# Two-layer transformer on one core: first-layer attention right behind the q/k projection, its output projection at the end of the same slot

## What is computed

```python
xn = layernorm(x)                                  # 8 x 256 x 256
x  = x + attn0(xn) + ffn0(xn)
xn = layernorm(x)
x  = x + attn1(xn) + ffn1(xn)

attn0: 16 heads of 128, biases on q, k, v, causal mask, softmax, output projection 2048 -> 256
ffn0:  float8 operands, gelu(gate) * linear, 1024 hidden
attn1: 16 heads of 16, no mask, output projection 256 -> 256
ffn1:  Walsh-Hadamard transform, up and gate projections, silu(gate) * up,
       transform, down projection (1024 hidden)
```

## Time and profile before

| | |
|---|---|
| runs (3) | 956.63, 958.75, 959.01 us; median 958.75 |
| profiled execution | 958.63 us, its span 956.8 us |
| first block | to about 144 us of the span |
| slots 3 to 127 | from 158.9 to about 852 us |
| mean granted TensorE clock | 0.937 |

### The profile page before, as it was taken

One profiled execution on the slowest core, in us unless ns is written; L12 is line 12 of the kernel. 1 busy time (PEld: TensorE's weight loads), 2 busy tenths in 40 slices (PEclk: granted clock), 3 DMA queues, 4 the chain that ended last, 5 costly groups with the idle time before them and its releaser, 6 DMA issues.

```text
span 956.8 us, 21194 instructions
## 1 busy us (share of the span) xinstructions
PE 830.6 (87%) x7120; PEld 609.9 (64%) x7120; DVE 742.3 (78%) x2028; ACT 689.1 (72%) x1973; POOL 471.4 (49%) x734
## 2 busy tenths in 40 slices
PE   3555538999899999999999999999999999996763
PEld 1123225687677777777777777777777777764541
DVE  6988855766768788887878787878787878875684
ACT  2654625656669778887888888788778878884673
POOL 1443332412326565665666555656565656566452
PEclk9675778999999999999999999999999999998896
DMA  9543412212243456554564555455556554544454
GB/s 331 196 148 110 133 52 82 52 34 43 48 103 75 90 93 140 102 83 108 123 105 78 115 116 111 77 124 102 107 80 143 89 101 89 123 98 93 114 107 102
DMA packets 283179, 100.97 MB, mean 106 GB/s; under 512 B 241344, under 2 KB 281024, under 8 KB 281920
## 3 DMA queue, kind: packets, MB, share of 16 engines
q1 hardware_dynamic: 280368, 97.27, 45.9%
q10 hardware_dynamic: 2704, 2.36, 0.7%
HBM read 30.38 MB, written 10.49 MB: 43 GB/s over the span
## 4 chain that ended last, share of the span: by engine, by line
PE 68%; DVE 9%; ACT 3%; issue 2%; DMA 1%; POOL 1%; SPq 0%; POOLq 0%; DVEq 0%; ACTq 0%
PE ps L666 42%; PE ps L716 9%; PE ps L816 4%; PE ps L799 4%; PE ps L692 3%; DVE arena L660 2%; PE ps L825 2%; PE ps L801 2%; PE ps L729 2%; DVE arena L999 1%; ACT arena L655 1%; DMA arena<-arena 1%; ACT arena L875 1%; DVE arena L659 1%; DVE nb L1006 1%
## 5 line engine op out<-in xcount | busy, mean ns | idle before, releaser
L660 DVE SCALAR_TENSOR_TENSOR arena<-ps,bqk,arena 128x256 bf16<-128x256 f32 x416 | 187.4, 479 | 63.3 <-ACT arena L655 61.8
L666 PE MATMUL ps<-arena,wqkv 128*128 128x256 bf16 x1728 | 215.2, 275 | 6.5 <-PEq L210 6.5
L655 ACT ACTIVATE arena<-ps,bqk 128x256 bf16<-128x256 f32 x416 | 177.9, 466 | 30.0 <-PE ps L666 20.8
L666 PEld LDWEIGHTS ps<-arena,wqkv 128*128 128x128 bf16 x1728 | 161.7, 98 | 48.1 <-issue 28.3
L1174 POOL TENSOR_SCALAR arena<-arena,rc 128x128 f32<-128x128 f32 (+1 forms) x256 | 106.3, 428 | 174.4 <-DVE rc L1022 174.4
L875 ACT ACTIVATE arena<-arena,nb 128x128 f32<-128x128 f32 (+1 forms) x256 | 114.3, 447 | 90.0 <-DVE nb L999 89.4
L1165 POOL TENSOR_TENSOR arena<-arena 128x512 bf16<-128x512 f32 x107 | 124.8, 1167 | 69.8 <-ACT arena L654 69.8
L1181 POOL TENSOR_SCALAR arena<-arena,rc 128x256 f32<-128x256 f32 x256 | 120.1, 483 | 75.7 <-DVE rc L1026 75.7
L654 ACT ACTIVATE arena<-arena 128x384 bf16<-128x384 f32 (+1 forms) x256 | 136.6, 572 | 18.7 <-POOL arena L1181 9.8
L875 ACT ACTIVATE arena<-ps,nb 128x256 f32<-128x256 f32 x256 | 118.6, 473 | 13.3 <-DVE nb L1006 10.8
L716 PE MATMUL ps<-wo,arena 128*128 128x256 bf16 x768 | 105.6, 274 | 10.5 <-DVE arena L660 9.8
(11 more groups left out here) (98 smaller groups left out, 1286.4 us busy)
## 6 DMA issues: line engine op xcount, KB each, us to landing
arena<-scratch_qk SPq DMA_DIRECT2D x96, 64.0 KB, 2.2
arena<-arena SPq DMA_TRANSPOSE x256, 2.7
scratch_qk<-arena SPq DMA_DIRECT2D x32, 128.0 KB, 1.9
arena<-in_x SPq DMA_DIRECT2D x4, 512.0 KB, 8.6
arena<-in_w_gating SPq DMA_DIRECT2D x2, 1024.0 KB, 6.7
arena<-in_w_q SPq DMA_DIRECT2D x2, 1024.0 KB, 8.6
scratch_xT<-arena ACTq DMA_DIRECT2D x8, 256.0 KB, 6.4
arena<-in_w_k SPq DMA_DIRECT2D x2, 1024.0 KB, 6.4
```

The costliest lines, as they stand in the source:

```text
L655: return nc.scalar.activation(out, in_, ACT.Identity, bias=bias)
L660: return nc.vector.scalar_tensor_tensor(out=out, in0=in_, scalar=bias, in1=hi, op0=ALU.add, op1=ALU.subtract)
L666: last = nc.tensor.matmul(out, lhsT, rhs, start=(n == 0), stop=(n == len(steps) - 1))
```

## The change

TensorE's loop calls attend0 directly behind the q/k projection, and project_out0 at the end of the slot, and now for the head of the same slot (`s - 3`, where it was `s - 4`). The evictions in between, o0_high and o0_low, go from the head of the slot on ScalarE and VectorE to a place behind the eviction of q and k. x1_sum, which needs the last output projection of a sequence, goes to the head of VectorE's slot. up_gate waits for x1T_lo itself, which the wait in project_out0 had implied.

```diff
@@ up_gate
                 upto(pe, v0_lo, min(s // 2 + 1, NG0 // 2))
+                pe.wait_ge(x1T_lo, b + 1)
@@ pe_program
                 if s < NG0:
                     proj_qk0(s)
-                if 0 <= s - 4 < NG0:
-                    project_out0(s - 4)
+                if 0 <= s - 3 < NG0:
+                    attend0(s - 3)
...
-                if 0 <= s - 3 < NG0:
-                    attend0(s - 3)
                 for n in quads_in[s]:
                     attend1(n)
                 for n in downs_in[s]:
                     down(n)
+                if 0 <= s - 3 < NG0:
+                    project_out0(s - 3)
@@ act_program
-                if 0 <= s - 4 < NG0:
-                    o0_high(s - 4)
...
                 if s < NG0:
                     qk0_high(s)
+                if 0 <= s - 3 < NG0:
+                    o0_high(s - 3)
@@ dve_program
-                if 0 <= s - 4 < NG0:
-                    o0_low(s - 4)
+                for b in x1_in[s]:
+                    x1_sum(b)
...
                 if s < NG0:
                     qk0_low(s)
+                if 0 <= s - 3 < NG0:
+                    o0_low(s - 3)
                 for n in heads_in[s]:
                     rec_1(n)
-                for b in x1_in[s]:
-                    x1_sum(b)
```

## The result

The changed kernel takes **1008.32 us**, the median of three runs (1008.04 to 1009.23), where the kernel before takes 958.75 (956.63 to 959.01). The ratio is 1.053, 95% interval 1.051 to 1.055: slower by about 50 us. The profiled execution spans 1006.5 us, against 956.8.

The account below looks back on a forecast made before the run. TensorE, its matmuls following without a hole from slot 28, was taken to bound the kernel. Terms 19.7 + 4.4 + 0.5 + 2.6 + 22.2 - 2.5 = 46.9, plus 3 for the clock, on 958.6 gave 1009 us; range 980 to 1031.

Parts of the forecast that it names:

- Q: Moment a slot's q/k projection has been issued; output projection cannot start before Q + 2.45 with layer-1 heads, Q + 2.64 without.
- The fold slots: Slots 3, 5, 7 and 8 to 15, with fold matmuls behind the output projection's wait: 6.83 us each.
- slots 3 to 15: Early slots where the output projection waits for evicted heads: 88.0 us instead of 68.3, +19.7.
- rival 1: Waits stay in early slots and are absorbed later, as weight loads leave TensorE room: 984 us, 13%.
- Slots 23 to 27: up_gate and layer-1 projection pieces fill 23, 24, 27; 25 and 26 wait: +0.5 us, bounds -1 and +3.
- Rounds: Slots 32 to 127, six rounds of 16: 3.7 us a round, +22.2 in all.
- Places 12, 14 and 15: Slots of a round: 12 and 15 wait 0.64 us each; in 14 ScalarE has o1_high first, 0.7.
- 0.3 goes with the removed waits at a slot's head: In each round, a gain of 0.3 us from waits removed at the slot's head.
- Place 10: Slot 10 of a round: attend0 waits 1.0 us for its transfer, swallowing the wait for o0_low.
- Tail: Slot 128's 1.95 us wait and half clock go, x1_sum no longer behind a reciprocal: -2.5 us (0 to -5).
- The clock: Two falls of TensorE's clock, 1.5 us each, between none and ten: +3 us.
- rival 2: Clock falls at each of ten long waits: 1021 us, or 1030 if TensorE stays at 1.2 GHz through some folds; 13%.

Follow-up runs that it names:

- The experiment with the fold ahead: Changed kernel with plain instead of transposing probability transfers and the up/down projections' fold before the output projection on TensorE: 983.6 us, 1.027 of the kernel before.
- The experiment with the early attention alone: Changed kernel with plain transfers, output projection back one slot later behind the q/k projection, x1_sum back behind rec_1: 963.7 us, 1.006 of the kernel before.
- The control: Kernel before, with each transposing transfer of the probabilities replaced by two plain ones of the same bytes: 956.2 us, 0.998 of the kernel before.

## Why the prediction was right

Forecast 1009 us, measured 1008.3, and the direction, the mechanism and the place of the loss are those of the prediction. That the total agrees within 1 us is partly luck: the clock cost 3.2 us more than forecast, and the rounds lost 3.5 us less.

- **The wait.** The output projection at Q + 2.64 without heads and Q + 2.45 with them: measured Q + 2.63 and Q + 2.40. The fold slots: 6.83 predicted, 6.85 measured; a slot of 28 to 31 was to take 4.69 + 0.64 = 5.33 and takes 5.30. The total of slots 3 to 15 without clock falls was to be 88.0 and is 88.2; slots 16 to 22 without theirs take 37.21 - 1.42 = 35.8, with 35.9 forecast. The experiment with the fold ahead shows that these waits are the cause: with a cover of 1.74 us, 18.1 us of them vanish. The issue intervals of the earlier trace rows decide, and the waits were not caught up in the rounds: the prediction's rival 1, which drew its room from the 3.89 us of weight loads, would have given 984. The rule of the Trainium skill on which it leaned ("Perfetto Trace Analysis", Identifying the Most-Contended Engine) is not borne out here as far as weight loads go: their busy time stood at 83% of the slot where TensorE had no room at all. That section of the Trainium skill names the share of the peak matmul rate beside weight-load time; the prediction read only the second, and no run here tests the first.
- **Slots 23 to 27**: +1.1 where +0.5 stood, inside its bounds. Slots 23 and 24 gained 0.39 and 0.61 us, 25 and 26 lost 0.63 and 0.31, as sketched. But slot 27, which was to be filled past the wait, lost 1.15 us: attention waits 1.21 us for its transfer there, a wait that the prediction had in the rounds only.
- **Rounds**: 3.1 us each instead of 3.7. Places 12, 14 and 15 came out as sized (0.62, 0.78, 0.60 against 0.64, 0.7, 0.64), and so did 11 (0.27 against 0.3), 3 (0.40 against 0.5), and 2, 6 and 9 together (0.34 against 0.2 for 2, 9 and 13). What failed is the last term, "0.3 goes with the removed waits at a slot's head": it was worth 0.55 in place 0 and 0.34 in place 4. Both could have been read in the kernel before. From slot 32 to 127 the matmuls of its output projection wait five times, always in place 0, and the lengths (0.53, 0.88, 0.54, 0.53, 0.53) are what the change won there (0.57, 0.92, 0.57, 0.57, 0.58). In place 4 of all six rounds its weight loads wait 0.34 us for o0_low. Place 10 came out at 0.99 against 1.0, in part by luck: five rounds lost 0.77 to 0.98 us, one 1.77, and in two of the six the wait was for o0_low and not for the transfer. The first wait in place 0, and the first in place 4:

```profile
398.97 0.83 PE L716 MATMUL ps<-wo,arena 128*128 128x256 bf16 x6 [0.53 <-DVE arena L660]
...
330.88 0.55 PEld L716 LDWEIGHTS ps<-wo,arena 128*128 128x128 bf16 x6 [0.34 <-DVE arena L660]
```

- **The second cause in the rounds.** The prediction put the waits for the transfer beside those for the eviction. The experiment with the early attention alone bears it out: such waits stay when the output projection's wait is gone. In the changed kernel they are 4.8 us in all between 340 and 905 us, about a quarter of the 18.7 us that the rounds lost.
- **Tail**: -1.3 instead of -2.5. The wait of 1.95 us at slot 128 and its clock fall were both to go. Neither did: in the changed kernel the output projection of that slot waits 1.40 us, and a fall of the clock follows. The control has the wait without a fall, so the fall was not a fixed part of that place. The tails of the five traces lie between 100.0 and 103.8 us, so a difference of 1.3 says little.

```profile
907.88 0.83 PE L716 MATMUL ps<-wo,arena 128*128 128x256 bf16 x6 [1.40 <-DVE arena L660]
...
910.00:913.00 3.00, 3.00 (x18) 2.10 (x16) 0.87 (x3) 1.48 (x6) 1.61 (x3) 0.55 0.90 230
```

- **The clock**: four falls of 1.06 to 2.03 us, 6.2 us in all, where two of 1.5 stood. The number of falls was the wrong step. The prediction's rival 2 (a fall at each of the ten long waits) did not come true either: in the timeline nine waits of the output projection between 170 and 290 us last 1.8 us or more, and four of them are followed by a fall. The prediction's "read strictly, every one of the ten would fall" took more from the Trainium skill than is there: its "TensorE: Matmul & The Clock Gate", Part 1, puts a condition on the idle time and does not say that every wait brings a fall.
- **"DVE arena L660" before L716** was to be some 75 us or more in over 100 places, and is 117.2 in 142. The bound held, but it was loose: the view counts weight loads and matmuls, each with its own wait.
- **Before slot 3** the changed kernel is 1.4 us ahead, of which nothing was forecast. The new order starts only there. The five traces, whose kernels have the same programs up to that point, reach slot 3 between 157.51 and 158.94 us, so 1.4 us is the scatter of that stretch and no effect of the change.

## What to carry to other kernels

A step that is moved nearer to what it waits for costs its whole latency less what stands between; find the moment at which its input can be there (here the q/k eviction's start plus two of its operations plus 0.54 us) and subtract, slot kind by slot kind, since the slots with a cover cost nothing. If such a step has to be near, put the slot's independent matmuls between (here the fold, worth 24.7 us by the medians, the 1.5 us of the plain transfers included). And when a step is moved forward, look at the transfer in front of it, on the queue where it stands behind others: that part of the loss remained here when the wait behind the step was gone.

## What the runs showed of the hardware that was not expected

- A wait of 1.8 to 2.0 us does not decide by itself whether the clock falls from 2.4 to 1.2 GHz. The place at slot 128, with 1.95 us of idle time and the same matmuls, fell to 0.53 in one execution and stayed at 1.00 in another. In the changed kernel four of nine such waits were followed by a fall; with the fold ahead, the three that remain (1.97, 1.81 and 1.98 us, between 230 and 260 us) were followed by none. The Trainium skill ("TensorE: Matmul & The Clock Gate", Part 1) says that idleness brings the throttled clock back; the four falls came right behind such waits and agree with it, and the five waits without a fall show that a wait of this length is not enough to forecast one. So a fall can be priced (1.06 to 2.03 us here), but from one trace of the kernel before their number could not be told; each count here is that of one execution.
- Two plain transfers in place of one transposing one land after a median of 2.0 us (1.9 to 5.2) instead of 2.6 (2.5 to 5.5), and changed no slot's length where nothing waited for them. The line of the transposing transfer in the changed kernel, then that of the plain ones in the last experiment:

```profile
DMA to landing us min/median/max: 2.5/2.6/5.5
```
```profile
DMA to landing us min/median/max: 1.9/2.0/5.2
```

- In both, single transfers took twice the median or more (5.5 against 2.6 us, 5.2 against 2.0). Attention waited up to 1.6 us for one, where the prediction had 1.0 from a landing of 2.5, and place 10 lost 0.8 to 1.8 us from round to round in the changed kernel, 0.2 to 1.8 with the early attention alone (there with plain transfers).
